# Joins of gathered expert rows spread over six blocks, and one down product moved ahead of the first block

## The reference

```python
x = _layernorm(x + _L0_attn_ref(x, Wk, Wv, Wo, gamma, beta))
x = _layernorm(x + _L0_ffn_ref(x, w_gate, w_gate_up, w_down, w_sh_gate_up, w_sh_down))
...
combine = jnp.sum(topk_w[..., None] * jax.nn.one_hot(topk_ids, E, dtype=x.dtype), axis=1)
gu = jnp.einsum('th,ehf->etf', x, w_gate_up)
act = _silu_and_mul(gu)
eo = jnp.einsum('eti,eih->eth', act, w_down)
routed = jnp.einsum('te,eth->th', combine, eo)
shared = _silu_and_mul(x @ w_sh_gate_up) @ w_sh_down
return (routed + shared).reshape(orig_shape)
```

## Time and profile before

| what | value |
|---|---|
| median of 3 runs | 696.09 us (695.78 to 697.63) |
| profiled execution, its own time | 695.84 us |
| its span | 694.0 us |
| PE, PEld busy | 662.5 us (95%), 527.6 us (76%) |
| DVE, ACT, POOL busy | 457.5 us (66%), 313.2 us (45%), 308.0 us (44%) |
| granted TensorE clock, mean over the span | 0.983 |

### The profile page before, as it was taken

One profiled execution on the slowest core, in us unless ns is written; L12 is line 12 of the kernel. 1 busy time (PEld: TensorE's weight loads), 2 busy tenths in 40 slices (PEclk: granted clock), 3 DMA queues, 4 the chain that ended last, 5 costly groups with the idle time before them and its releaser, 6 DMA issues.

```text
span 694.0 us, 16580 instructions
## 1 busy us (share of the span) xinstructions
PE 662.5 (95%) x6792; PEld 527.6 (76%) x6792; DVE 457.5 (66%) x796; ACT 313.2 (45%) x544; POOL 308.0 (44%) x314
## 2 busy tenths in 40 slices
PE   9999999999999999999999999999999977999993
PEld 7767777677777777878887888888887865887882
DVE  6874954967745562598845654455457876788875
ACT  5243543454554531421133655665567533354523
POOL 0757567577555341011024443543353354565714
PEclk9999999999999999999999999999999996999997
DMA  8213235132624241100265577864679444423313
GB/s 280 93 28 95 65 98 140 51 111 80 206 90 112 79 140 47 30 1 0 70 226 161 184 242 274 299 215 155 225 256 351 167 115 116 133 77 120 95 45 121
DMA packets 66575, 93.53 MB, mean 135 GB/s; under 512 B 17024, under 2 KB 32128, under 8 KB 66496
## 3 DMA queue, kind: packets, MB, share of 16 engines
q1 hardware_dynamic: 60816, 73.81, 32.3%
q0 software_dynamic: 5680, 18.62, 9.6%
HBM read 68.61 MB, written 23.79 MB: 133 GB/s over the span
## 4 chain that ended last, share of the span: by engine, by line
PE 66%; DVE 15%; POOL 7%; issue 7%; ACT 4%; DMA 1%; DVEq 0%; POOLq 0%; ACTq 0%
PE bank L1343 8%; PE bank L1194 6%; PE zbank L1417 6%; PE wbank L1417 6%; PE bank L1454 6%; PE zbank L1331 4%; PE bank L1249 4%; PE zbank L1302 3%; PE wbank L1302 3%; PE wbank L1331 3%; PE zbank L1430 2%; PE bank L1302 2%; PE wbank L1228 2%; PE zbank L1212 2%; POOL za L2035 2%
## 5 line engine op out<-in xcount | busy, mean ns | idle before, releaser
L2067 POOL TENSOR_TENSOR xl<-RAW,xh 128x1024 fp32r<-128x1024 f32 x23 | 56.3, 2449 | 122.2 <-ACT xh L1874 122.1
L1950 ACT ACTIVATE ah<-sg 128x512 fp32r<-128x512 f32 x36 | 22.7, 632 | 113.7 <-DVE sg L1605 113.7
L2084 POOL DMA_INDIRECT xg<-x1d,idxu x39 | 42.1, 1079 | 71.1 <-DVE idxu L1002 41.3
L1595 DVE TENSOR_TENSOR GL<-RAW,GH 128x1024 fp32r<-128x1024 f32 x36 | 43.3, 1225 | 11.0 <-ACT GH L1869 9.5
L2109 POOL DMA_INDIRECT xg<-yd,SI x32 | 32.9, 1027 | 36.1 <-DVE x L1729 30.5
L1194 PE MATMUL bank<-xh,GH 128*128 128x512 f32 x112 | 47.8, 427 | 0.8 <-DVE kS L1495 0.8
L1681 DVE TENSOR_TENSOR x<-bank,x 128x512 f32<-128x512 f32 x64 | 42.5, 682 | 8.4 <-PE bank L1343 8.3
L1343 PE MATMUL bank<-xh,ah 128*128 128x512 f32 x112 | 45.5, 406 | 1.9 <-DVE x L1681 1.0
L1194 PE MATMUL bank<-xl,GH 128*128 128x512 f32 x112 | 44.2, 394 | 0.2
L1343 PE MATMUL bank<-xl,ah 128*128 128x512 f32 x112 | 44.2, 394 | 0.0
L1343 PE MATMUL bank<-xh,al 128*128 128x512 f32 x112 | 44.1, 394 | 0.0
(11 more groups left out here) (366 smaller groups left out, 1991.4 us busy)
## 6 DMA issues: line engine op xcount, KB each, us to landing
RAW<-in_wgu SPq DMA_DIRECT2D x13, 1024.0 KB, 6.1
yd<-RAW SPq DMA_DIRECT2D x39, 256.0 KB, 5.1
RAW<-in_wsgu SPq DMA_DIRECT2D x14, 512.0 KB, 5.2
RAW<-in_wd SPq DMA_DIRECT2D x13, 512.0 KB, 5.9
xr<-in_xT SPq DMA_DIRECT2D x16, 256.0 KB, 4.3
x<-in_xtok SPq DMA_DIRECT2D x16, 256.0 KB, 4.0
x1d<-x SPq DMA_DIRECT2D x16, 256.0 KB, 2.8
RAW<-in_wsd SPq DMA_DIRECT2D x8, 512.0 KB, 4.4
```

Source lines behind the costliest of these rows:

```text
L1595: e.tensor_tensor(GL[:, w % 2, k:k + 2, :], gate_raw(w, k), GH[:, w % 2, k:k + 2, :].bitcast(F32), ALU.subtract).then_inc(*mark("low", "g" ...
L2067: e.tensor_tensor(DL[:, w % 2, :, :], draw[:, raw_of(w), :, :], DH[:, w % 2, :, :].bitcast(F32), ALU.subtract).then_inc(*mark("low p", "d" ...
L2084: e.indirect_dma_start(place(s), None, x1d, bass.IndirectOffsetOnAxis(ap=idxu[:, LINES[s]:LINES[s] + 1], axis=0)).then_inc(*mark(f"dma xg{ ...
```

## The change

The joins of tiles 0 and 1 stay in the last ordinary group. Join 2 goes behind "pair split" T3, and joins 3 to 15 are dealt out by a new table over blocks 2 to 7, as are the finishes of tiles 0 to 7. Finish 0 now stands in block 2; blocks 3 and 5 have three joins and no finish; block 7 has finishes 5, 6 and 7 and join 15. The first of block 2's four down products is issued ahead of the block's product 1, and its addition on DVE ahead of the split of T3. No computation is added or taken away: 32 join instructions, 32 gathers, 16 finishes and the same matmuls.

```diff
--- before.py
+++ after.py
@@ -558,19 +558,21 @@
     split_down(BASE + 1)
     do("load down", BASE + 2)
     for step, _ in enumerate(gate(BASE, 3)):
-        if step % 2 == 0:
+        if step in (0, 2):
             join(step // 2)
+    early = pair_down(0, 2)
+    next(early)
     do("pair split", "T3", gate_end[BASE])
+    join(2)
     do("pair split", "T4", None)
-    join(4)
-
-
-    side = {(2, 3): "j5", (2, 4): "j6", (3, 1): "f0", (3, 3): "j7", (3, 4): "j8", (4, 1): "f1", (4, 5): "f2", (4, 3): "j9", (4, 4): "j10",
-            (5, 1): "f3", (5, 5): "f4", (5, 3): "j11", (5, 4): "j12", (6, 1): "f5", (6, 5): "f6", (6, 3): "j13", (6, 4): "j14",
-            (7, 1): "f7", (7, 3): "j15"}
+
+
+    side = {(2, 1): "f0", (2, 3): "j3", (2, 4): "j4", (3, 1): "j5", (3, 3): "j6", (3, 4): "j7", (4, 1): "f1", (4, 5): "f2", (4, 3): "j8", (4, 4): "j9",
+            (5, 1): "j10", (5, 3): "j11", (5, 4): "j12", (6, 1): "f3", (6, 5): "f4", (6, 3): "j13", (6, 4): "j14",
+            (7, 1): "f5", (7, 5): "f6", (7, 3): "j15", (7, 4): "f7"}
     for b in range(2, 8):
         u = b // 2
-        downs = pair_down(u - 1, 2 + b % 2)
+        downs = pair_down(u - 1, 2 + b % 2) if b > 2 else early
         for p in block(b, (1, 5, 6, 2, 7, 3, 4)):
             if p == 1 and b < 7:
                 after = mul_end[b - 1] if b > 2 else gate_end[BASE]
```

## The result

| | before | with the change |
|---|---|---|
| median of 11 runs each, on one chip | 695.72 us | 692.37 us |
| lowest to highest | 693.60 to 697.63 | 689.88 to 694.32 |
| ratio, 95% interval | | 0.9949 [0.9934, 0.9963] |
| the profiled execution: time, span | 695.84, 694.0 | 689.88, 688.1 |

The change is faster, as forecast, by 3.4 us (2.6 to 4.6 by the interval), where 7.7 were forecast, and 692.37 lies above the range's end of 691.0. The profiled execution is the shortest of its eleven: by it alone the gain would be 5.96 us.

A forecast was written before the change was run, and what follows sets the result against it. PE was held by a stall in block 2 behind DVE's joins, then by half clock. 6.34 + 1.37 + 2.45 = 10.16 us, less 1.2 (clock), 0.5 (block 3), 0.8 (tail), gave 7.7: 688.2 us from 695.84, range 686.2 to 691.0.

The forecast's parts named there:

- The stall in front of block 2: Block 2: with the joins out of the group, product 6 starts 6.34 us earlier; PE idles 2.8 us instead of 8.8.
- Rival 3: Block 2: the early down finds bank 4 or inputs late, PE waits before product 1, nothing won, 695.8 us; chance 0.04.
- The down product, 1.37 us: Block 2: one down group moved ahead of product 1 leaves one fewer behind product 6; block 3 starts 1.37 us earlier.
- Block 3, a wait of 0.5 us: Block 3: DVE's chain to add 5 grows 1.6 us against 1.1 slack, so PE waits 0.5 us at product 3.
- costed at nothing: Items given no time, among them SP issuing the first output tile ahead of the last unit's weights, needed three blocks later.
- rival 4: Blocks 2, 3, 5: late gathers for joins 2, 5 and 10 hold DVE and stop PE; slower, 698.2 us; chance 0.03.
- signs of being wrong: Product 6 starting later than 576, DVE waiting for gathers in blocks 3 to 7, or a block over 16 us.
- The clock, 2.45 gone and 1.2 given back: Behind product 6 of block 2: half speed costing 2.45 us goes; 1.2 given back, the middle of 0 and 2.45.
- The tail, 0.8 us: Block 7: DVE sets the end, so finish 7 behind product 4's low part costs its full 0.8 us.
- block 5, nothing: Block 5: a join replaces two finishes, nothing gained or lost; the 0.3 us wait for add 5 stays.
- Rival 1: Block 2: the clock stays low as long as before, 3.9 us given back instead of 1.2, 690.9 us; chance 0.10.
- Rival 2: Blocks 3 and 5: joins meet POOL's low-weight subtraction, two meetings of 0.65 us, 689.5 (693.0 by the skill's rule); chance 0.13.

The follow-up runs named there:

- e8: The changed kernel with the down product back behind product 4 of block 2, joins as changed; 690.55 us, 0.9943 of the kernel before.
- e7: The kernel before with only the down product moved ahead of product 1, joins left in the group; 693.46 us, 0.9977 of the kernel before.
- e2: The changed kernel with the last unit's weight loads put ahead of output 0 on SP; 689.34 us, 0.9909 of the kernel before.
- e11: The changed kernel with finish 0 moved from block 2 to behind add 5 of block 3; 689.98 us, 0.9928 of the kernel before.
- e10: The kernel before with unread matmuls filling PE's idle times, 28 ahead of product 5 and 6 ahead of product 6 of block 2; 694.07 us, 0.9985.
- e12: The changed kernel with ten unread matmuls ahead of product 6 of block 2 and ten ahead of product 3 of block 3; 690.22 us, 0.9926.
- e5: The changed kernel with finish 7 moved from behind product 4 to behind product 7 of block 7; 689.91 us, 0.9930 of the kernel before.
- e3: The changed kernel with the splits of T3 and T4 and join 2 moved behind ACT's copy 1 of block 2; 690.85 us, 0.9933.
- e4: The changed kernel with both the edits of e2 and e3; 688.40 us, 0.9898 of the kernel before.
- e1: The changed kernel unaltered, run and profiled again; 691.34 us, 0.9946 of the kernel before.
- e9: e2 with ten unread matmuls between products 5 and 6 of block 2; 687.95 us, 0.9894 of the kernel before.
- e6: e4 with finish 0 in block 3, finish 7 behind product 7, and DVE's low part of block 3's weights behind the weight sums; 685.43 us, 0.9861.

## Why the forecast was right in direction and wrong in size

**The stall in front of block 2: right.** Product 6 was to start at 574.24 and started at 574.58, which is 574.27 without the 0.31 us by which this execution was late; the idle time was to be 2.8 us and is 2.67. Product 5 was to come at about 570.1 and came at 570.39. Rival 3 (the stall is not moved) is out.

**The down product, 1.37 us: right for the start of block 3, worth nothing that could be told at the end.** Block 3 did start at 585.59, of 585 forecast. But where DVE sets product 3's moment, PE's lead turns into PE's wait, and e8 without this edit is as fast. In the kernel before, where nothing waits in block 3, the same edit is worth 1.6 us (e7).

**Block 3, a wait of 0.5 us: this step failed.** It rested on "it comes just in time" for join 5, with 5.5 us on either side and landings of 3.9 at most, and on the output tile ahead of the loads "costed at nothing". DVE reached join 5 5.6 us behind join 3's end, as forecast; what failed is the landing. I asked only when the loads' consumer needs them and not beside whom they run. Timelines of SP and of POOL before:

```profile
587.57 0.38 SPq L1098 DMA_DIRECT2D RAW<-in_wsgu  x1
```
```profile
584.52 0.94 POOL L2109 DMA_INDIRECT xg<-yd,SI  x1 [0.30 <-issue]
```

There the loads went out 8 us ahead of block 3, and the gathers nearest to them at 584.52 and at 595.87, with a join waiting for neither; now they are issued at 586.18, in block 3's first microsecond, and 1.35 us ahead of join 5's gathers. A wait of 2.70 us came, with the block 3.1 us longer instead of 0.5: **2.6 us of the missing 4.3**. Moving the loads (e2) or what stands ahead of them (e11) takes that wait down to 0.71 and 0.26. It is rival 4's mechanism at one of its three places, at 6.2 us of landing; that rival even said that the weights' DMAs "now fall nearer to join 5". I gave it 0.03 because I looked at the whole of it, three late joins, and not at the one without slack. Two of the prediction's signs of being wrong came with it: DVE waited for gathers in block 3, and the block took 18.15 us, over 16.

**The clock, 2.45 gone and 1.2 given back: this step failed too.** It treated the half speed as a fixed cost of the kernel before and the 1.2 as a middle between two ends. The 2.45 is right for the execution that was profiled (e10 takes 2.35 us of it away), but both kernels have executions that pay and executions that do not. Before lost 1.0 to 1.5 us by it over all its executions (ratio and median of e10), not 2.45, and the changed kernel loses about 1.5 as well (e12). The term's net of +1.25 us was about nothing. That a half clock behind PE's idleness is what costs the time is shown by e10 and e11; the sizes over all executions are less sure than those of block 3's wait.

With both corrected the sum is 7.7 - 2.6 - 1.25 = 3.85 us, of 3.4 to 3.7 measured. By the executions without the clock's loss it closes as well: the forecast without its clock term was 6.34 + 1.37 - 0.5 - 0.8 = 6.4, less 2.6 is 3.8; from e10 to e12 it is 694.07 - 690.22 = 3.85. That it closes to the last digit is luck, as each of these medians is good to about 1 us and the two ran on different chips; and block 3's wait, taken from one profile at 2.70, was 1.72 to 2.82 in others.

**The tail, 0.8 us, and block 5, nothing: right** (0.80 by e5; a wait of 0.18 us in block 5, where 0.3 was before).

**Rival 1** (the clock stays low through block 2) was not seen in the six profiles that have this gap of 2.6 to 2.9 us and no filler: one (e11) shows 3.4 us at half speed, five none. **Rival 2** (more joins meet POOL's subtraction) did not happen: two pairs of joins took 2.21 and 2.23 us instead of 1.60, as two did before (2.25 and 2.26). But its price of 0.65 us a meeting is not the price of a meeting; it is what was left of POOL's instruction when the join began. Those four began with 0.82 to 0.86 us of POOL's 2.4 left and lost 0.61 to 0.66; e3's subtraction began with 2.36 left and lost 2.2. The trace of before had the full price in it too, at joins 0 and 1, four instructions that take 3.2 us elsewhere:

```profile
561.56 5.26 DVE L1729 SCALAR_TENSOR_TENSOR x<-xg,WW,x 128x512 f32<-128x512 f32 x4
```
```profile
561.41 2.48 POOL L2067 TENSOR_TENSOR xl<-RAW,xh 128x1024 fp32r<-128x1024 f32 x1 [2.38 <-ACT xh L1874]
```

They began with 2.33 us of POOL's left and lost 2.1.

What stays open is why the same 2.7 us of idleness is followed by half speed in some executions and not in others, and why block 3's wait was 2.70 in one profile and 1.72 in the next. No run here tells.

## What to carry to other kernels

When work is taken out of a stretch, everything behind it comes nearer, transfers too: for each transfer with no slack, list which other transfers are issued in the 5 us around it in the new order, not only when its own consumer needs it (loads 1.35 us ahead of the gathers cost PE 2.7 us here, loads 5.1 us ahead, in e4, nothing). A product taken off PE's path is worth its time only up to the next place where another engine sets the moment. And an idle time can cost more than its length, through the clock behind it; the scatter between executions hints at it, and filling the gap with matmuls that nobody reads measures it.

## What was unexpected of the hardware

- A gather of 3.6 us in the median took up to 6.2 us while 1.5 MB of weights were loading and the DMA share was 0.90 to 1.02.
- An idle time of PE of about 2.7 us was followed by 3.4 us at 1.2 GHz in one profile (e11) and by a full clock in five (the changed kernel, e1, e2, e5, e8). Executions of one program differed by 2 to 4 us, and by 1 us or less with PE kept at work (e9, and e12 but for one run).
- An elementwise instruction of DVE or POOL that began while one of the other engine ran lost what was left of that one, less 0.15 to 0.3 us: 0.6 of 0.8, 2.1 of 2.3, 2.2 of 2.4 us on DVE, and 0.48 of 0.63 on POOL (e6). All of these have two inputs in SBUF.
- In e7 PE ran product 5 at half speed behind its stall and product 6 at full speed; in the profile of before product 6 and the down product behind it were at half speed too.
